# Attention of a transformer layer: GpSimd normalises the context, both halves of a pair's sum in one visit, value tiles spread over the lead

## The reference

```python
def _L0_attn_ref(x, Wq, Wkv, Wo, bo):
    B, T, D = (1, 512, 1024)
    H, G = (32, 8)
    HD = D // H
    REP = H // G
    ...
    scores = jnp.einsum('bhqd,bhkd->bhqk', q, k)
    causal = jnp.triu(jnp.ones((t, t), dtype=bool), 1)
    scores = jnp.where(causal[None, None], -jnp.inf, scores)
    weights = jax.nn.softmax(scores * (1.0 / HD ** 0.5), axis=-1)
    ctx = jnp.einsum('bhqk,bhkd->bhqd', weights, v)
    ctx = ctx.transpose(0, 2, 1, 3).reshape(b, t, d)
    return jnp.dot(ctx, Wo) + bo
...
x = x + _layernorm(_L0_attn_ref(_layernorm(x, axis=-1), L0_attn_Wq, L0_attn_Wkv, L0_attn_Wo, L0_attn_bo), axis=-1)
```

## Time and profile before

| what | before |
|---|---|
| median of 3 runs | 2858.45 us |
| the profiled execution, its own time | 2857.54 us |
| its span | 2855.7 us |
| PE busy over the span | 2725.0 us (95%) |
| DVE, ACT, POOL busy | 1281.1, 887.8, 1016.2 us |
| granted TensorE clock, mean | 0.982 |
| steps of `attend`, first to last exp | 320.4 to 1248.3 us |

### The profile page before, as it was taken

One profiled execution on the slowest core, in us unless ns is written; L12 is line 12 of the kernel. 1 busy time (PEld: TensorE's weight loads), 2 busy tenths in 40 slices (PEclk: granted clock), 3 DMA queues, 4 the chain that ended last, 5 costly groups with the idle time before them and its releaser, 6 DMA issues. The chain is left out here.

```text
span 2855.7 us, 42146 instructions
## 1 busy us (share of the span) xinstructions
PE 2725.0 (95%) x17472; PEld 1157.6 (41%) x17472; DVE 1281.1 (45%) x1627; ACT 887.8 (31%) x1591; POOL 1016.2 (36%) x554
## 2 busy tenths in 40 slices
PE   6999899999999999989959999999999998999998
PEld 3445433333333333324424444444444443444443
DVE  6332777778778787616652322332233221010001
ACT  3111366666666666650011111111111111000000
POOL 0000276676766767742223232233323320010001
PEclk9999999999999999999979999999999999999999
DMA  4222101101011010022232322233223223224220
GB/s 169 78 77 88 29 16 31 42 16 29 16 44 29 16 29 2 2 82 89 89 99 74 92 80 80 81 92 82 78 85 86 78 74 123 70 81 127 69 69 29
DMA packets 200761, 187.15 MB, mean 66 GB/s; under 512 B 22416, under 2 KB 175504, under 8 KB 200592
## 3 DMA queue, kind: packets, MB, share of 16 engines
q1 hardware_dynamic: 200592, 184.76, 21.0%
HBM read 134.74 MB, written 49.81 MB: 65 GB/s over the span
## 5 line engine op out<-in xcount | busy, mean ns | idle before, releaser
L730 POOL TENSOR_TENSOR c_prob<-c_prob 128x1024 f32<-128x1024 f32 (+1 forms) x288 | 604.6, 2119 | 512.4 <-ACT c_prob L626 509.9
L642 DVE TENSOR_REDUCE c_maxes<-c_s 128x2 f32<-128x1024 f32 (+3 forms) x640 | 645.7, 1058 | 189.9 <-PE c_s L482 189.4
L626 ACT ACTIVATE c_prob<-c_s 128x512 f32<-128x512 f32 (+1 forms) x1152 | 598.0, 571 | 324.0 <-PE c_s L504 185.0
L504 PE MATMUL c_s<-c_q,c_k 97*128 97x512 f16 (+3 forms) x1280 | 368.7, 354 | 8.6 <-ACT c_prob L626 0.6
L1182 POOL TENSOR_TENSOR e_hl<-e_h,e_hh 128x512 f16<-128x512 f32 (+1 forms) x88 | 120.9, 1374 | 492.0 <-ACT e_hh L1153 492.0
L519 PE MATMUL c_ctx<-c_prob,v_sb 128*32 128x512 f32 (+3 forms) x2560 | 295.1, 542 | 0.2 <-ACT c_c L615 0.2
L1073 PE MATMUL e_gp<-x_hi,e_w_hi 128*128 128x512 f16 x704 | 267.8, 380 | 20.8 <-DVE e_w_lo L1105 20.8
L1126 DVE SCALAR_TENSOR_TENSOR e_h<-e_up,e_silu 128x512 f32<-128x512 f32 x84 | 58.1, 692 | 493.3 <-PE e_up L1075 493.3
L1074 PE MATMUL e_gp<-x_lo,e_w_hi 128*128 128x512 f16 x704 | 267.6, 380 | 0.0
L1075 PE MATMUL e_gp<-x_hi,e_w_lo 128*128 128x512 f16 x704 | 267.6, 380 | 0.0
L1074 PE MATMUL e_up<-x_lo,e_w_hi 128*128 128x512 f16 x672 | 254.7, 379 | 0.0
(11 more groups left out here) (134 smaller groups left out, 3064.7 us busy)
## 6 DMA issues: line engine op xcount, KB each, us to landing
h_hi<-e_hh SPq DMA_DIRECT2D x84, 128.0 KB, 1.8
h_lo<-e_hl SPq DMA_DIRECT2D x84, 128.0 KB, 1.8
f_h_hi<-h_hi SPq DMA_DIRECT2D x7, 1344.0 KB, 8.5
f_h_lo<-h_lo SPq DMA_DIRECT2D x7, 1344.0 KB, 6.9
b_x<-L_attn_x SPq DMA_DIRECT2D x16, 512.0 KB, 6.5
c_q<-qk_hi SPq DMA_DIRECT2D x64, 128.0 KB, 3.0
d_x<-L_attn_x SPq DMA_DIRECT2D x16, 512.0 KB, 4.9
x_dram<-d_x SPq DMA_DIRECT2D x16, 512.0 KB, 2.6
```

The costliest lines, as they stand in the source:

```text
L504: last = nc.tensor.matmul(S2[:, h % 2, at:at + w], K[:, g % 2, k * P:(k + 1) * P], Q[:, g % 2, b, h, q:q + w], start=True, stop=not diag)
L626: nc.scalar.activation(prob(g, s, 0, w)[:, h, :], S2[:, h % 2, 0:w], ACT.Exp, scale=exp_scale).then_inc(exp_done, 1)
L642: last = nc.vector.tensor_reduce(MAXES[:, g % 2, t // TPB, heads, t % TPB, u], S1[:, heads, at:at + w], AX.X, ALU.max)
L730: return nc.gpsimd.tensor_tensor(one, one, two, ALU.add)
```

## The change

Four edits, all in `attend`:

1. Both halves of the 12 pairs have place a + 4.
2. `invert_piece` has two pieces: the turn, and in the next step the inverse and the spread together. The multiplication with the context moves to GpSimd, at the head of `cut_context`, and CN has one buffer in place of two.
3. GpSimd calls `cut_context` ahead of the first pair of a block: ahead of pair 0 for block 2 of the group before, ahead of pair 3 for block 3 of the group before, ahead of pair 10 for block 0 and ahead of pair 21 for block 1.
4. The value tiles' 24 halves in the lead are spread over all 17 visits, one or two behind each.

```diff
         for a in range(first, last - 2, 2):
-            sums += [(b, a, a + 1, 0, a + 3), (b, a, a + 1, 1, a + 4)]
+            sums += [(b, a, a + 1, 0, a + 4), (b, a, a + 1, 1, a + 4)]
...
                 visit(0, v)
-                for _ in range(min(2, len(halves))):
+                while len(halves) > (2 * NT - 2 * EARLY) * (LEAD - 1 - v) // LEAD:
                     half_value_tile(*halves.pop(0))
...
-                elif i == 1:
+                else:
                     dve.wait_ge(sum_read, n + 1)
                     nc.vector.reciprocal(RT[:, :], ST[:, 0:BANK:HD]).then_inc(inverted, 1)
-                elif i == 2:
                     dve.wait_ge(inverted, n + 1)
                     if n:
                         dve.wait_ge(normed, n)
                     nc.vector.transpose(R[:, :], RT[:].rearrange("p (c o) -> p c o", o=1)
                                         .broadcast_to([P, BANK // HD, HD])).then_inc(spread, 1)
-                else:
-                    if n >= 2:
-                        dve.wait_ge(ctx_lo_done, n - 1)
-                    dve.wait_ge(ctx_read, n + 1)
-                    dve.wait_ge(spread, n + 1)
-                    nc.vector.tensor_tensor(CN[:, b % 2, :], C[:, b % 2, :], R[:], ALU.mult).then_inc(normed, 1)
...
+                pool.wait_ge(ctx_read, n + 1)
+                pool.wait_ge(spread, n + 1)
+                if n:
+                    pool.wait_ge(ctx_lo_done, n)
+                nc.gpsimd.tensor_tensor(CN[:, :], C[:, b % 2, :], R[:], ALU.mult).then_inc(normed, 1)
                 pool.wait_ge(normed, n + 1)
-                nc.gpsimd.tensor_copy(c_hi[:, g, at], CN[:, b % 2, :]).then_inc(ctx_hi_done, 1)
+                nc.gpsimd.tensor_copy(c_hi[:, g, at], CN[:, :]).then_inc(ctx_hi_done, 1)
...
+            cut_at = {0: [(-1, 2)], 1: [(-1, 3)], 2: [(0, 0)], 3: [(0, 1)]}
             for g in range(GROUPS):
...
                 for a, c in pairs:
-                    if a in cuts:
-                        cut_context(*cuts[a])
+                    b = steps[a][0]
+                    if a == first_of[b]:
+                        for earlier, of in cut_at.get(b, []):
+                            if g + earlier >= 0:
+                                cut_context(g + earlier, of)
                     add_pair(g, a, c)
+            cut_context(GROUPS - 1, NB - 2)
             cut_context(GROUPS - 1, NB - 1)
```

More of the change, by code:

```diff
@@ L392, in attend @@
         MROW = sb("mrow", [TPB * REP, P], F16)
-        C, R, CN = sb("c", [P, 2, BANK]), sb("r", [P, BANK]), sb("cn", [P, 2, BANK])
+        C, R, CN = sb("c", [P, 2, BANK]), sb("r", [P, BANK]), sb("cn", [P, BANK])
         ST, RT = sb("st", [P, BANK]), sb("rt", [P, BANK // HD])
@@ L701, in _ @@
                         i = s - last_of[b] - 3
-                        if 0 <= i < 4:
+                        if 0 <= i < 2:
                             invert_piece(g, b, i)
-                        elif g and 0 <= i + STEPS < 4:
+                        elif g and 0 <= i + STEPS < 2:
                             invert_piece(g - 1, b, i + STEPS)
@@ L713, in _ @@
                                 join_maxima(g + ahead, b)
-            for i in range(4):
+            for i in range(2):
                 invert_piece(GROUPS - 1, NB - 1, i)
@@ L743, in add_pair @@
                     add(g, a, c, 3 * P, BANK, 0).then_inc(added, 1)
+            cut_at = {0: [(-1, 2)], 1: [(-1, 3)], 2: [(0, 0)], 3: [(0, 1)]}
             for g in range(GROUPS):
-                cuts = {}
-                for b in range(NB):
-                    ready = last_of[b] + 6
-                    if ready < STEPS:
-                        cuts[min(a for a, _ in pairs if a + 2 >= ready)] = (g, b)
-                    elif g:
-                        cuts[min(a for a, _ in pairs if a + 2 >= ready - STEPS)] = (g - 1, b)
-                for a, c in pairs:
-                    if a in cuts:
-                        cut_context(*cuts[a])
+                for a, c in pairs:
+                    b = steps[a][0]
[3 more added lines that the diff above has]
+                                cut_context(g + earlier, of)
                     add_pair(g, a, c)
+            cut_context(GROUPS - 1, NB - 2)
             cut_context(GROUPS - 1, NB - 1)
```

2 lines of the change are left out of this document (1 added, 1 removed).

## The result

The changed kernel takes 2879.51 us, the median of 5 runs (2874.12 to 2882.01), beside 2858.45 us for the kernel before on the same chip. The ratio is 1.0068, with a 95% interval of 1.0054 to 1.0082: it is slower, by 21.1 us. The forecast was 2873, from 2862 to 2884. The direction was right, and so in the main was the mechanism. The size was 6.5 us short, and most of what follows is about those.

A forecast was written before the change was run, and what follows sets the result against it. It took a ring of ScalarE's exps and TensorE's scores to bound the steps. Terms 28.9 - 11.6 - 2.7 + 2.5 - 1.5 - 0.4 + 0.6 = +15.8, less 1, gave 2873 us, range 2862 to 2884.

The forecast's parts named there:

- the ring: Steps of `attend`: a score needs the PSUM bank read by the exp two heads back, an exp needs its score.
- The asymmetry that the forecast rests on: Steps of `attend`: a second half of sums costs 0.43 us, a left out half gives back 0.08.
- Edit 1, +28.9: Sums of 12 pairs a group: an empty and a double step cost 0.36 us more than two single ones; +28.9 together.
- the 0.2 taken off at each diagonal: Steps 15, 19, 26: longer diagonal work fills part of the empty step's wait, so 0.2 us less for each.
- Edits 2 and 3: Step 6's wait for GpSimd goes, -11.6 us; L691 gone, -2.7; earlier spread on VectorE, +2.5; low clock avoided, -1.5.
- Edit 4: Lead: better pace but later first exp, net +1.3 us; low clock after it regained, 1.7; -0.4 together, -3 to +2.
- The end: End of the stage: last cut takes 3.1 us on GpSimd in place of 0.68 on VectorE and 1.85; +0.6.
- the 1 for shared steps: Steps 6 and 7: where two losses share a step one hides part of the other, so 1 us off.
- (a): Pairs: the empty step gives back all it loses on TensorE, -13.4 in place of 28.9, 2831 us; 5 in 100.
- (b): Pairs cost nothing: the empty step gives back as much as the double one takes, 2844 us; 6 in 100.
- (c): Pairs cost the last group's 0.18 us everywhere, 2861 us; 7 in 100.
- (d): Empty steps' waits bring the clock down, 1.5 us a fall, one a group making 2885 us; 7 in 100.

The follow-up runs named there:

- shorter maxima: Changed kernel with VectorE's reductions of full visits for the maxima on 384 of 512 columns, exps full: 2860.65 us, ratio 1.0005.
- shorter exps of heads 0 and 1: Changed kernel with exps of heads 0 and 1 on 384 of 512 columns in full-width steps without sums: 2879.32 us, ratio 1.0072.
- shorter exps of heads 2 and 3: Changed kernel with exps of heads 2 and 3 on 384 of 512 columns in full-width steps without sums: 2874.90 us, ratio 1.0057.
- one half left out: Kernel before, with the first half of each of a group's 12 pairs never summed: 2841.06 us, ratio 0.9940.
- the third piece: Kernel before with edits 2 and 3 alone, but VectorE's inverse and spread in steps of their own again: 2842.15 us, ratio 0.9946.

## Why the prediction was right, and where it was 6 us short

**What bounds a step.** Right in the main. Four exps in one row every second step and L504 0.88 long behind an empty step stand in the changed kernel, and the third exps come at 2.9 and more in turn. The double steps are not all at the 3.4 of the forecast: they lie between 3.17 and 3.95. And the forecast had ScalarE's four exps as the bound of an empty step; only two of them are on it. That the exps of heads 2 and 3 are the ring is shown by shortening them (2.88 to 2.67, to the hundredth) and by shortening the other two (nothing). The asymmetry that the forecast rests on is measured twice more: 2.88 and 3.07 in the last group, and 2.88 and 3.40 where VectorE is fast enough (steps 13 and 14 with the shorter maxima).

**Edit 1, +28.9.** This is the term that was mis-sized: it measures 33.9 us, 32.4 of them in the steps (7 groups of 4.16 and 3.3 in the last, forecast 3.7 and 2.9). The term had nothing for VectorE. What the forecast said of VectorE stood beside edit 2: 0.53 to spare in an empty step, against 0.24 + 0.70 of pieces, and what is left reaches the next visit "by some 0.05 each". The first half of that is right and the second is not. The pieces make the reductions of step 13 start 0.30 late. But from a visit to the end of its reductions it is 0.43 + 2.36, and the next visit's second half waits for that end, so in a step of 2.88 hardly 0.1 of the delay is absorbed: 0.22 come out in step 14. With edit 1 undone step 13 is 0.09 longer, and 0.13 come out. The second half of step 14's visit starts 3.22 behind the third exp of step 13 in both kernels: there VectorE sets the time.

In the changed kernel VectorE's share, by the run with shorter maxima, is 0.21 to 0.34 in each of steps 9, 14, 20, 25 and 35, 0.08 in 16 and 27, and next to nothing in the other double steps with a visit. The forecast had named visits that wait for VectorE by more than 0.3 in steps 13, 14, 24 and 25 as a sign of being wrong. Half of that came: 0.22 in step 14 and 0.34 in step 25. How much of edit 1's cost is VectorE's can only be bounded: at most 1.2 of the 4.16 a group (the 1.95, less what step 4 and the fused piece have in any case), since edit 1 undone and with shorter reductions was not run. That leaves at least 2.9 a group for the ring, where the forecast had 3.7. So the near hit may in part be luck: 0.36 a pair was read at one place, and if VectorE's share is near its bound, that was too much for the ring elsewhere, and what VectorE added made up for it. A second point in the same term: the 0.2 taken off at each diagonal was right for steps 15 and 26 (0.18 a pair measured) and wrong for step 19 (0.37), behind which VectorE adds 0.34 in step 20.

**Edits 2 and 3.** -12.1 measured, -12.7 forecast. The stall of step 6 goes wholly (4.88 to 3.14), the wait behind L691 in step 9 is worth 0.50 in six groups (0.45 in six forecast), the multiplication takes 1.27 on GpSimd (1.16 forecast) and hides as said. The fused piece costs 3.7 to 4.2 and not 2.5, again through VectorE: 0.13 and 0.18 in steps 14 and 25 in place of 0.05, and 0.19 in step 4 in place of 0.25. The stretch of low clock behind the stall is gone, which is worth 1.0 (1.5 forecast).

**Edit 4.** -0.4 forecast; +1.2 alone, with an interval of -1.1 to +4.0 (the ratio's, times 2858), and -0.7 between the medians with and without it beside edits 2 and 3. Its two parts have the sign and about the size forecast, 1.5 lost and 2.3 regained, but the second is read in the fastest execution. In the changed kernel's profiled execution the gain isn't whole: 3.4 us of low clock lie in its first steps, from 324.3, and cost 1.5: group 0 takes 119.22 there and 117.69 with the shorter exps of heads 0 and 1, where the clock holds and the other groups are the same. Of the five profiled kernels with edit 4 and full reductions two have such a fall in the first steps (the changed one and that with shorter exps of heads 2 and 3), three have none, and nothing here tells why.

**The end.** +0.6 forecast. From the last exp to the first matmul of the projection it is 1.2 longer, two times as much. Busy time by engine of that stretch and of the one behind it, before and then after, with the granted clock as the third number from the end:

```profile
1247.95:1262.71 14.76, 2.56 (x40) 0.84 (x33) 3.65 (x6) 3.09 (x5) 4.79 (x4) 0.74 0.35 120
1262.71:1280.00 17.29, 17.29 (x75) 7.60 (x76) 8.51 (x7) 7.62 (x7) 0.00 (x0) 0.92 0.59 232
```

```profile
1268.38:1284.38 16.00, 2.79 (x49) 1.20 (x41) 2.96 (x5) 3.09 (x5) 9.05 (x8) 0.65 0.30 112
1284.38:1301.67 17.29, 17.29 (x67) 7.25 (x68) 8.48 (x7) 7.63 (x7) 0.00 (x0) 0.83 0.58 231
```

TensorE waits through that end, and the projection begins at a lower clock, 0.83 in place of 0.92: in the same 17.29 us it does 67 matmuls where it did 75. The low clock there lasts 10.2 us before, 17.1 after, and 13.7 with edit 1 undone. It is 13.7 in all five kernels that have edit 2 without edit 1, but also in one without edit 2 (one half left out) and in three that have both. That the longer end prolongs it fits in part, and isn't shown. The projection as a whole takes 2.0 longer, with 5.9 in place of 2.7 us of it at the low clock, and no term stood for that.

**The sum.** Forecast were -12.7 (edits 2 and 3), -0.4 (edit 4) and +27.9 (edit 1 less the 1 for shared steps), +14.8. Measured from kernel to kernel: -12.1, -0.7 and +33.9, +21.1. Nearly all of the gap, 6.0 of 6.3, is in edit 1.

**The rivals.** (a), TensorE's work as the price, and (b), an empty step that gives back what the double one takes, fell with the steps of 2.88, with edit 1 undone and with the half left out. The rule of the Trainium skill on which (a) drew ("TensorEngine Tiling (Array Packing)", section "Tiling Modes": a change of mode drains TensorE) isn't refuted: the 0.14 a pair is there in the changed kernel too (1.00 for both halves, 0.57 for one). That it is a drain no run here shows. It is TensorE's time, and in the pairs the empty step doesn't give back TensorE's work. (c), 0.18 everywhere, holds in the last group's steps without visits and at two diagonals, no further. (d), a fall of the clock at the empty steps, didn't come: from 327.7 us to the last exp there is no low clock.

## What to carry to other kernels

Work that is moved from one step to another in a ring of two engines must be priced by the distances of an empty, a single and a double step, as they stand in the trace (2.88, 2.97 and 3.40 here), not by the busy time of the work (0.57). Here the first unit of work in a step costs 0.08 to 0.16 in most (up to 0.40 at a diagonal), the second its whole 0.43: so spread it evenly. That gave 2836.8 us where bundling gave 2879.5; of the 42.7 between them, 33.9 are the pairs, 5.3 the halves at the blocks' ends and 4.2 the third piece, with 0.7 the other way for edit 4. And before a step is priced as shorter or a piece put into it, the next slowest engine's spacing from hand-over to hand-over belongs beside it: an engine that is busy in 74% of a stage (VectorE) still added 0.21 to 0.34 to five of the steps behind a short one.

## What the runs showed that was not expected

Shortening something on the bound can give next to nothing although the bound is right: two exps shorter by 0.21 together made 15 steps of a group shorter by 0.21 each, and the group as a whole by 0.5.

The clock can fall in the middle of a busy stage. In the kernel before it does, once, behind the stall of step 6 in group 4; with edit 4 alone it falls at the same place in group 3. Busy time by engine and clock of that stretch there, the columns as in the earlier trace rows:

```profile
691.40:694.80 3.40, 3.40 (x20) 0.70 (x16) 0.32 (x1) 1.77 (x4) 3.40 (x3) 0.50 0.02 5
```

TensorE had waited 1.65 us for GpSimd, up to 689.8. The granted clock is 0.50 (1.2 GHz) for the 3.4 us from 691.4, which cost that group 1.04 (117.64 and 116.60). The same wait stands in seven groups and the fall comes in one, so the wait alone doesn't bring it; that the fall comes of it isn't shown. In none of the kernels without this stall is there a fall within `attend` behind its first steps.

Apart from a few places, step times repeat to the hundredth between groups 1 to 6, and between kernels wherever the code around a step is the same (step 12 at 2.88, step 14 at 2.97). A difference of 0.05 in one step is therefore a finding, though the whole kernel's time can't be told to better than 5.7 us.
